# Row blocks between the products of the next tile, products as couples of half-row passes, without filler waits

## What is computed

```python
Kf  = jnp.einsum('bjd,ed->bje', F, K_w)      # F: 2048 x 64 x 128, K_w and Q_w: 128 x 128
S   = jnp.einsum('bid,bjd->bij', F, Kf)      # per b a 64 x 64 matrix
out = jnp.einsum('bij,ijd->bid', S, W)       # W: 64 x 64 x 128, shared by all b
out = out + jnp.einsum('bid,ed->bie', F, Q_w)
```

## Time and profile before

| | us |
|---|---|
| median of 3 runs | 607.61 (606.63 to 608.42) |
| the profiled execution, its own time | 606.42 |
| its span, first to last instruction | 604.6 |
| TensorE matmuls busy | 596.4 (99%) |
| VectorE, ScalarE busy | 399.2, 401.5 (66% each) |
| HBM read and written | 69.86 and 67.11 MB |

### The profile page before, as it was taken

The page is one execution under the profiler, slowest core; times in us unless marked ns, Lnnn a source line. Parts: engine busy times, 40 slices in busy tenths (PEclk is TensorE's granted clock), DMA queues, the critical chain, the costliest instruction groups (busy, mean ns, idle before and its releaser), DMA issues.

```text
span 604.6 us, 17904 instructions
## 1 busy us (share of the span) xinstructions
PE 596.4 (99%) x7690; PEld 526.3 (87%) x7690; DVE 399.2 (66%) x412; ACT 401.5 (66%) x696; POOL 0.2 (0%) x4
## 2 busy tenths in 40 slices
PE   9999999999999999999999999999999999999995
PEld 7888989889898898988989898898988989889895
DVE  6556768567685675947749475685756768567486
ACT  7888393874938659295692947939387493865920
POOL 0000000000000000000000000000000000000000
PEclk9999999999999999999999999999999999999999
DMA  8644847457575575755657566484754857557177
GB/s 338 262 141 160 330 165 282 183 185 305 191 281 172 210 266 208 279 196 210 242 192 287 203 238 249 143 319 174 277 209 173 318 179 284 173 209 273 70 281 279
DMA packets 29452, 138.12 MB, mean 228 GB/s; under 512 B 3264, under 2 KB 3776, under 8 KB 21312
## 3 DMA queue, kind: packets, MB, share of 16 engines
q1 hardware_dynamic: 20736, 75.83, 31.8%
q10 hardware_dynamic: 8640, 61.15, 28.4%
HBM read 69.86 MB, written 67.11 MB: 227 GB/s over the span
## 4 chain that ended last, share of the span: by engine, by line
PE 98%; DVE 1%; issue 1%; DVEq 0%
PE ps L509 20%; PE ps L447 20%; PE ps L449 19%; PE ps L448 19%; PE ps L541 18%; DVE o_sb L372 1%; PE ps L576 1%; DVEq L49 0%; DVE o_sb L382 0%; PE ps L467 0%; PE ps L465 0%; PE ps L469 0%; DVE f_hi L388 0%; DVEq L115 0%
## 5 line engine op out<-in xcount | busy, mean ns | idle before, releaser
L337 DVE TENSOR_TENSOR f_lo<-f_ring,f_hi 128x1024 fp32r<-128x1024 f32 x124 | 151.8, 1224 | 168.2 <-ACT f_hi L217 166.6
L231 ACT ACTIVATE q_out<-ps 128x512 f32<-128x512 f32 x256 | 156.9, 613 | 6.6 <-PE ps L449 0.2
L222 ACT ACTIVATE kf<-ps 128x512 f32<-128x512 f32 x256 | 155.8, 609 | 3.5
L372 DVE TENSOR_TENSOR o_sb<-ps,q_out 128x1024 f32<-128x1024 f32 x127 | 145.1, 1215 | 19.4 <-PE ps L541 19.3
L240 ACT ACTIVATE s_t<-ps 128x512 f32<-128x512 f32 x32 | 19.1, 598 | 175.8 <-PE ps L509 175.8
L509 PE MATMUL ps<-f_ring,kf 128*64 128x64 f32 x4096 | 123.5, 222 | 0.3 <-issue 0.3
L509 PEld LDWEIGHTS ps<-f_ring,kf 128*64 128x64 f32 x4096 | 121.1, 138 | 2.6 <-issue 0.8
L541 PEld LDWEIGHTS ps<-s_t,w_sb 64*128 64x128 f32 x2048 | 115.6, 188 | 5.6 <-issue 5.6
L541 PE MATMUL ps<-s_t,w_sb 64*128 64x128 f32 x2048 | 118.6, 274 | 0.0
L447 PE MATMUL ps<-f_hi,k_hi 128*128 128x512 f32 x255 | 101.0, 396 | 0.0
L447 PE MATMUL ps<-f_hi,q_hi 128*128 128x512 f32 x256 | 100.0, 391 | 0.0
(11 more groups left out here) (39 smaller groups left out, 160.3 us busy)
## 6 DMA issues: line engine op xcount, KB each, us to landing
out<-o_sb SPq DMA_DIRECT2D x127, 512.0 KB, 3.5
f_ring<-f_t ACTq DMA_DIRECT2D x58, 1024.0 KB, 4.8
f_ring<-f_t SPq DMA_DIRECT2D x4, 1024.0 KB, 10.6
f_ring<-f SPq DMA_DIRECT2D x8, 256.0 KB, 5.3
w_sb<-w SPq DMA_DIRECT2D x1, 2048.0 KB, 17.8
out<-o_sb SPq DMA_DIRECT2D x2, 256.0 KB, 2.6
o_sb<-first SPq DMA_DIRECT2D x1, 192.0 KB, 2.9
o_sb<-first ACTq DMA_DIRECT2D x1, 192.0 KB, 3.4
```

Of the source, the lines that this page charges most:

```text
L222: nc.scalar.activation(kf[:, c // 2, c % 2 * CK:(c % 2 + 1) * CK, :, :].rearrange("d k h i -> d (k h i)"), ps[:, 2 * c % 8, :], COPY).then ...
L231: nc.scalar.activation(q_out[:, t % 2, :, :].rearrange("d i (h b) -> d i h b", h=2)[:, :, :, at:at + CK], q_bank(t * CHUNKS + c).rearrange ...
L337: nc.vector.tensor_tensor(f_lo[:, v % SPLIT, :], f_unit(v), f_hi[:, v % SPLIT, :].bitcast(F32), ALU.subtract).then_inc(flo_done, 1)
L372: nc.vector.tensor_tensor(o_sb[:, n % OBUF, :, :, :].rearrange("d x s b -> d s x b"), ps[:, bank:bank + 2, :].rearrange("d s (x b) -> d s ...
```

## The change

In the products of tiles 1 to 15, each pass of 128 rows is replaced by two of 64 rows, on the lower and the upper half of the partitions. `first_halves(step)` makes the lower half of the K product and the upper half of the Q product, matmul by matmul in turn; `second_halves(step)` makes the other halves into the same banks, and waits first (`half_done`) that the first halves of that step have ended. TensorE's order is first halves of step n, second halves of step n-1, and so on. K and Q products of a step now end together. The filler waits go.

The row blocks of tile t-1 stand in the middle of the products of tile t, behind both halves of step 7 (`MID` is 8). Row block k (k below 4) waits for the copies of step 4+k, and steps 8 to 11 wait for sums 4 to 7 of the row blocks. The scores wait for the copies of steps 12 to 15.

On VectorE the eight sums stand between low v+5 and both v+6 and not behind low v+9. The splits wait for K products too. In the last tile the last step is a couple of K products of chunks 14 and 15.

```diff
-FILL = {1: 0, 2: 56}
-FILL.update((t, 108) for t in range(3, TILES - 1))
-FILL[TILES - 1] = 132
+MID = 8
...
                 act.wait_ge(q_done, 2 * (v - SPLIT) + 2)
+                act.wait_ge(k_done, 2 * (v - SPLIT) + 2)
...
                 low_f(v + 3)
                 both_f(v + 4)
                 low_f(v + 5)
+                for k in range(UNITS):
+                    sum_out(t, k)
                 both_f(v + 6)
                 low_f(v + 7)
                 both_f(v + 8)
                 low_f(v + 9)
-                for k in range(UNITS):
-                    sum_out(t, k)
...
+            def products(step):
+                if step < TILES * CHUNKS - LATE:
+                    return (q_of(step), q_done), (k_of(step), k_done)
+                return (k_of(step), k_done), (k_of(step + 1), k_done)
...
+            def passes(dst, w_hi, w_lo, c, rows, first):
+                hi = f_hi[rows, c // 2 % SPLIT, piece_cols(c)]
+                lo = f_lo[rows, c // 2 % SPLIT, piece_cols(c)]
+                yield nc.tensor.matmul(dst, w_hi[rows, :], hi, start=first, stop=False)
+                yield nc.tensor.matmul(dst, w_hi[rows, :], lo, start=False, stop=False)
+                yield nc.tensor.matmul(dst, w_lo[rows, :], hi, start=False, stop=not first)
+
+            def first_halves(step):
+                (a, _), (b, _) = products(step)
+                for ins_a, ins_b in zip(passes(*a, lower, True), passes(*b, upper, True)):
+                    pass
+                ins_a.then_inc(half_done, 1)
+                ins_b.then_inc(half_done, 1)
+
+            def second_halves(step):
+
+                pe.wait_ge(half_done, 2 * (step - CHUNKS + 1))
+                (a, a_sem), (b, b_sem) = products(step)
+                for ins_b, ins_a in zip(passes(*b, lower, False), passes(*a, upper, False)):
+                    pass
+                ins_b.then_inc(b_sem, 1)
+                ins_a.then_inc(a_sem, 1)
...
-                        pe.wait_ge(kf_copied, (t + 1) * CHUNKS + 13 + k)
-                        pe.wait_ge(q_copied, min((t + 1) * CHUNKS + 13 + k, TILES * CHUNKS - LATE))
+                        pe.wait_ge(kf_copied, (t + 1) * CHUNKS + MID - 3 + k)
+                        pe.wait_ge(q_copied, (t + 1) * CHUNKS + MID - 3 + k)
...
+                    if t >= 1 and MID <= c < MID + 4:
+
+                        pe.wait_ge(out_done, (t - 1) * UNITS + 5 + c - MID)
+                    elif c >= 4:
+
+                        pe.wait_ge(kf_copied, n - 2 if n == TILES * CHUNKS - LATE else n - 3)
...
+                    if (4 <= c < MID or c >= MID + 4) and n < TILES * CHUNKS - LATE:
+                        pe.wait_ge(q_copied, n - 3)
+                    first_halves(n)
+
+                    if c >= 1 and c != MID:
+                        second_halves(n - 1)
+                    if c == MID - 1:
+                        second_halves(n)
+                        rows_tile(t - 1)
+                if t >= 1:
+                    second_halves(min((t + 1) * CHUNKS - 1, TILES * CHUNKS - LATE))
```

More of the change, by code:

```diff
@@ L208, in split_first @@
                 wait(act, q_done, 2 * (c // 2 - SPLIT) + 2)
+                wait(act, k_done, 2 * (c // 2 - SPLIT) + 2)
                 nc.scalar.activation(f_hi[:, c // 2 % SPLIT, piece_cols(c)], f_cols(c), COPY).then_inc(fhi_first, 1)
@@ L225, in copy_q @@
             def copy_q(t, c):
-                act.wait_ge(q_done, t * CHUNKS + c + 1)
+                n = t * CHUNKS + c
+                act.wait_ge(q_done, n + 1 if n < TILES * CHUNKS - LATE else TILES * CHUNKS)
                 if c == 0:
@@ L328, in both_first @@
                 wait(dve, q_done, 2 * (c // 2 - SPLIT) + 2)
+                wait(dve, k_done, 2 * (c // 2 - SPLIT) + 2)
                 if c == 4:
@@ L470, in k_halves @@
                 ins.then_inc(k_done, 1)
[L472 to L498, removed]
             def scores(t, e):
@@ L514, in scores_tile @@
                 for e in range(UNITS):
[L515 to L526, removed]
+                    pe.wait_ge(kf_copied, t * CHUNKS + max(2 * e + 2, 13 + e // 2))
+                    if e % 2:
+                        pe.wait_ge(q_copied, min(t * CHUNKS + 13 + e // 2, TILES * CHUNKS - LATE))
+                    if t == 0 and e == 0:
+                        for c in range(2):
+                            pe.wait_ge(f_first[c], 16)
                     scores(t, e)
@@ L571, in rows_tile, with project @@
                     row_block(t, k)
+            def project(t):
+                for c in range(CHUNKS):
+                    n = t * CHUNKS + c
+                    if n == TILES * CHUNKS - 1:
+                        break
+                    if n == 0:
+                        k_halves()
+                        pe.wait_ge(qlo_done, 1)
+                        q_product(n)
+                        continue
+                    if n < PIECES:
+                        pe.wait_ge(flo_first, n + 2)
+                    elif n % 2 == 0:
+                        pe.wait_ge(flo_done, n // 2 - FIRST + 1)
+                    if t >= 1 and MID <= c < MID + 4:
+                        pe.wait_ge(out_done, (t - 1) * UNITS + 5 + c - MID)
+                    elif c >= 4:
+                        pe.wait_ge(kf_copied, n - 2 if n == TILES * CHUNKS - LATE else n - 3)
+                    elif t >= 1:
+                        pe.wait_ge(s_copied_act if c % 2 else s_copied, (t - 1) * 2 + c // 2 + 1)
+                    if t == 0:
+                        k_product(n)
+                        if c >= 4:
+                            pe.wait_ge(q_copied, n - 3)
+                        q_product(n)
+                        continue
+                    if (4 <= c < MID or c >= MID + 4) and n < TILES * CHUNKS - LATE:
+                        pe.wait_ge(q_copied, n - 3)
+                    first_halves(n)
[6 more added lines that the diff above has]
+                    second_halves(min((t + 1) * CHUNKS - 1, TILES * CHUNKS - LATE))
             pe.wait_ge(zeros_done, 1)
```

11 lines of the change are left out of this document (9 added, 2 removed).

## The result

The changed kernel takes 624.25 us (median of 6 runs, 623.02 to 627.55), the kernel before 607.14 us (6 runs, 606.63 to 608.42): a ratio of 1.029, 95% interval 1.026 to 1.032. It is slower by 17.1 us. The forecast, 614.5, had the sign, and the range, 601 to 627, holds the time; but the forecast loss was 7.4 us against a measured 17.1.

A forecast was written before the change was run, and what follows sets the result against it. TensorE, busy 99% of the span, was taken as the bound. Its own 36.35 us plus 0.77 (sums), 0.25 (stores) and 0.1 (holes) gave 37.47 a tile against 36.96, +7.6 over 15 tiles: 614.5, range 601 to 627.

The forecast's parts named there:

- X: Products of tiles 1 to 15: time of one couple of two half-row matmuls, taken as 0.222 us.
- the late stores: Row blocks' sums waiting for store buffers while a load runs beside the stores: 0 to 0.5 us a tile, taken as 0.25.
- 75 X + 20.47: Formula for a tile's time in us before s is added; only 75 of 96 couples still move the end.
- s: Time a tile loses to stores and instruction holes, added to 75 X + 20.47; 0.35 us in the forecast.
- Turns: TensorE's changes between kinds of tile: products to row blocks and back cost nothing; 0.40 instead of 0.56 us a tile.
- Waits for sums: Behind the row blocks TensorE waits 0.17 us for sum 4, 0.46 for sum 5; VectorE sets step 12; cost 0.77 a tile.
- Filling: Removing filler waits from TensorE's queue: filler itself costs nothing; without it instruction holes of 0 to 0.8 us a tile, taken 0.1.
- the filling was worth its place: Rival on removing the filler: 0.4 us a tile more than the forecast took, 620 us; chance 0.07.
- the couples are light: Rival on the products: X = 0.217, s = 0, waits seen at once, -0.40 us a tile, 601.6 to 604; chance 0.24.
- the bubble goes: Rival on the products: X = 0.2158 while the waits come, 37.00 us a tile, no change, 608.1; chance 0.14.
- Their own surcharge: Rival on the products: couples cost extra, X = 0.235, 38.4 to 38.5 us a tile, 630 us; chance 0.10.
- The halves don't run together: Rival on the products: a couple's two matmuls don't overlap, 21.8 us more a tile, over 900 us; chance 0.01.

The follow-up runs named there:

- the first experiment: The changed kernel with 216 filler waits a tile put back between product steps, so instruction fetches fall at the same places of every tile: 622.05 us, ratio 1.024.

## Why the prediction was right or wrong

Two terms of the sum were too small: the couples' pitch X (0.222, measured 0.2267) and the late stores (0.25 a tile, measured 0.71). The rest of the sum held.

**The couples' pitch: mis-sized.** I took X = 0.222, midway between an estimated pass with nothing around it and the full passes; it is 0.2267, the row nearest by columns and operands. The lower bound came from matmuls in the warm-up, scaled to the full clock, and no row at the full clock had it. The prediction's own formula, 75 X + 20.47, gives 37.47 with the measured X and s = 0; the quiet tile takes 37.51. So all but X and s was right to 0.04 us, in part by luck: with the dearer couples TensorE's own path reaches step 12 at the same time as VectorE's. The step costs 75 x 0.0047 = 0.35 a tile, 5.3 us. The Trainium skill, page "TensorE: Matmul & The Clock Gate", Part 1, with some 0.216 for a warm pass, isn't borne out: full, half and single passes of 512 columns all stand 0.227 apart. Nor is its Part 3, that a load overlaps only where the row group differs: full passes and couples have one pitch, and the loads are hidden in both. No surcharge by the Trainium skill's span model (the same Part 3), a few ns for each further tile in the array, shows in the pitch either: it is the same with and without a partner.

**Turns: right.** Products to row blocks follows at the pitch, and products to scores costs 0.14 (0.31 from start to start and a first score of 270 ns), where I had 0.17. The couples in the old order, which spare the turn from products to row blocks alone, give 0.17 a tile, against 0.19 by the rows.

**Waits for sums: right.** The sums start 1.41 behind the first row matmul by the forecast, 1.48 (236.97 to 238.45) by the trace. The wait for sum 4 is 0.23, and 0.08 of an unhidden load come to it: 0.31 where I had 0.17 in all. That for sum 5 is 0.27 + 0.11 = 0.38 (0.46). Together 0.69 against 0.63. Unit 6's low half ends at 12.49 (12.41), and step 12 starts at 12.63 (12.58). A wait of its own doesn't show there, as with the dearer couples TensorE comes no earlier. Moving the split by 1.86 us cost 19 us: 15 x (1.86 - 0.76) = 16.5, where 0.76 is what the late stores of a tile cost less, and 2 more in two tiles whose row blocks took longer (9.70 and 10.84 instead of 9.23). That bears the chain out.

**Stores: the mechanism right in half, the size wrong.** I had the load beside the stores, the three sums with least to spare, and 0 to 0.5 us a tile, and took 0.25. It is 0.71 as a mean, 1.28 at the most. What failed is the bound: the spare time was computed from bytes and rate, and a fetch of 16 KB on one engine adds 1.1 to 1.5 us to one sixteenth of a store, for which the whole buffer waits. With the load gone early the wait is 1.1 us in all, with the fetch in the wrong place 12.4. The row of fetches stood in the profile, and I read it for TensorE's own holes alone.

**Filling: the mechanism wrong, the size right by luck.** I gave 0.1 a tile for holes in TensorE's instructions. That they are late blocks was read rightly, but they come in the old order; in the changed one the scores have none. What the filling did was to hold the fetches in place. The rival "the filling was worth its place" (620, chance 0.07) was nearest to the time and wrong in its mechanism: putting filling back wins 2 to 3 us, 0.15 to 0.2 a tile, and not 6, since in the couples' order it costs 0.3 to 0.4 a tile itself. Tile 2's product stage of 22.24 could have warned me that filler isn't free at each place: without its filler the same stage takes 22.01.

**The sum.** 0.35 for X, 0.40 for s (0.75, that is 0.71 and the 0.04 above, instead of 0.35), together 0.75 a tile, 11 us over 15 tiles; measured less forecast is 9.8, with the last tiles less late than the mean. For the rivals: against "the couples are light" and "the bubble goes" stands the pitch; they needed X below 0.220 and at 0.2158. "Their own surcharge" (0.235) falls by the same row. "The halves don't run together" falls by the common starts.

**What stays open:** why a fetch makes a part 1.5 us late, where 16 KB at one engine's share of the measured rate (1/16 of 406 GB/s) are 0.65 and the fetch itself took 1.06; I made no run with another size. What made a part late in three tiles without a fetch in the time: 83.4 above, 310.0 with half stores (2.1 us), and by 0.8 one of full passes without filling. Why the clock fell with single half-row passes. And full passes with the row blocks in the middle and the load early, the best of both findings, weren't run; by the busy times they would still owe the 0.21 of turns.

## What to carry to other kernels

When stores and a large load meet, size the slack of a buffer for its latest sixteenth and not for the bytes: a 16 KB fetch of instructions on one DMA engine makes the whole store late. (Pieces of 8 KB, 0.31 us long, did not: with one at 4.4 us in the tile at 122.6 of the first experiment all 16 parts landed by 6.71.) The number of instructions in a loop body sets where these fetches fall, so a change of that number moves time between places that have nothing to do with it; align it, test the kernel with the fetch moved, or move the load (here one line for 7.4 us). And price a matmul by the nearest row of the same columns at the full clock: cutting a pass of 512 columns into two half-row partners neither cost nor won anything but turns here, while asking for its operands earlier can cost a wait.

## What the runs showed of the hardware that I had not expected

- A 64-row pass of 512 columns in this float32 form starts 0.227 us behind the last one, alone, with a partner on the other row half, or as a full pass of 128 rows.
- One 16 KB instruction fetch makes one of 16 parts of a 512 KB store land up to 1.5 us behind the rest beside a load of F (1.9 in other runs), and 1.7 in a tile where the store is 256 KB; its place alone is worth 14.6 us in 622.
- When 256 short matmuls (0.03 us each) and their weight loads run while stores fill the DMA, a late block of instructions stops TensorE for 0.3 to 1.0 us, until 1.3 to 1.7 us behind the end of a fetch.
- Waits on a semaphore long set are free only while TensorE has matmuls queued: behind a wait that ends just in time, or behind short scores, they cost about 0.1 us each in the first case and up to 1.0 us in seven instructions in the second.
- With half of the rows in use in the products, in one run, the granted clock was 0.90 as a mean, though TensorE was busy for 97% of the span.
